# Feed-forward halves joined, the last layer's rounding shared with GpSimd and its last tile halved, the first ternary weights turned by DMA

## The chip, the core and the metric

The kernel runs on one core of a Trainium2 chip. Its engines run side by side, each with an instruction queue of its own: TensorE (PE, matrix products and transposes), VectorE (DVE), ScalarE (ACT), GpSimd (Pool) and SyncE (SP, which here only issues DMA transfers). They wait for each other through semaphores. The metric is the device time of one execution, in microseconds; lower is better.

## The reference, cut

Four transformer layers over x (4 x 256 tokens, D = 256), each an attention-like block and a feed-forward block behind a layer norm:

```python
x = x + _L0_xattn_ref(_layernorm(x), token ids, ctx, ctx, ctx)   # l0x: gated experts chosen by token id
x = x + _L0_ffn_ref(_layernorm(x), w1, w3, w2)                   # l0: ternary weights, SiLU gate
x = x + _L1_xattn_ref(..., w, u, _layernorm(x), ctx)             # wkv: a recurrence along the tokens
x = x + _L1_ffn_ref(_layernorm(x), ...)                          # l1 (shared expert) and the MoE
x = x + _L2_xattn_ref(_layernorm(x), ctx, ...)                   # l2x: attention on quantised values
x = x + _L2_ffn_ref(_layernorm(x), w1, w2, w3)                   # l2: ternary weights, sigmoid gate
x = x + _L3_xattn_ref(_layernorm(x), ctx, ...)                   # l3x: linear attention
x = x + _L3_ffn_ref(_layernorm(x), gate_w, up_w, down_w)         # l3: block-quantised to fp8 steps
```

Ternary weights are `clip(round(w / mean(abs(w))), -1, 1)`, so -1, 0 or 1 times one scale. The last layer quantises activations and weights in blocks of 32:

```python
def _mx_dequant(t):
    blocks = t.reshape(rows, feat // 32, 32)
    scales = maximum(max(abs(blocks), -1) / 448, 1e-30)
    q = (blocks / scales[..., None]).astype(float8_e4m3fn).astype(float32)
    return (q * scales[..., None]).reshape(rows, feat)
gate = _mx_linear(x2d, gate_w); up = _mx_linear(x2d, up_w)
out = _mx_linear(silu(gate) * up, down_w)        # the hidden values are quantised again
```

## The kernel before

Activations stand turned (D on the partitions, 1024 tokens along the row) and are worked on in two halves of 512 tokens. The code is a program written out by hand for each engine; the order in it is the order in which that engine runs, and each engine's queue is strictly in order.

**Feed-forward blocks.** `ffn(s)` stands once for each of PE, ACT and DVE and serves l0x (8 units a half), l0 (6), l1 (3) and l2 (6). A unit i is 128 rows of the hidden layer: PE makes the two products w1 and w3 (below: w(i)), ACT applies the activation, DVE multiplies (`gate`), and PE's `down(i)` adds the unit's share of the output in PSUM banks 4 and 5. `down` lags behind w by `lag` units: 1, or 2 in the blocks in `SPLIT` (l0, l2). There the activations are cut into a high part (ACT, `hidden_high`, `ln_high`) and a low part (DVE, `hidden_low`, `ln_low`) and each product is made with both. A half ends with its last `lag` down products; then DVE adds the output to x (`add_y`, which increments `x_ready`), and only behind that does PE begin the next half. `down(0)` of a half waits for the addition of the half before, since it overwrites the banks.

**Norms inside.** The layer norms of the next half and of the next block's first half are done inside a block, in steps placed by `ln_steps` at given units: PE makes the mean, DVE subtracts (`xc`), ACT squares (`sq`), PE makes the variance (`var`), ACT the root (`sd`, with a table load of 1.28 us each way), DVE `diag`, PE `rows`, DVE `xn`, and in split blocks ACT and DVE the two `parts`.

**Ternary weights.** `ternary` is a list of pieces that DVE runs between the units of l0x (for l0) and of the MoE (for l2): absolute sums, and from piece 7 on the codes, written over the fp32 weights. For l0, PE then turns the weights with 36 transposes behind l0x (`pe_turn(pe, "l0")`), while ACT and DVE copy them out of PSUM in turn (`copy_out`). For l2, Pool casts the codes to bf16 behind DVE's last piece, SP issues three DMA transposes, and ACT copies the results into place behind the attention, ahead of l2.

**Last layer.** 1024 tokens are 8 tiles of 128. DVE's `mx_quant` is a chain: block maxima (tensor_reduce), scale, reciprocal, multiplication, the exponent bits by a tensor_scalar, another tensor_scalar, then an addition and a subtraction of a power that round, and a multiplication back. The tokens of the first half are quantised at once, those of the second in two pieces of two tiles, behind product(1) and product(2). For the hidden values of tile t, PE makes gate and up (`gate_up(t)`), ACT the SiLU, DVE `product(t)` and the chain up to the rounding, Pool the multiplication back (L893), PE turns them (`hidden_turned(t)`), ACT copies them (`hidden_copied`), PE makes `down(t)`, DVE adds the residual (`result(t)`) and SP stores. PE's order is hidden_turned(t), down(t-1), gate_up(t+2); all down products use bank 6, so down(t) waits for result(t-1).

## Time and profile before

| | us |
|---|---|
| median of three runs | 1064.69 |
| lowest, highest | 1057.3, 1065.52 |
| the profiled execution | 1067.97 |
| its span, first to last instruction | 1066.2 |
| PE busy | 874.2 |
| DVE busy | 737.8 |
| ACT busy | 459.8 |
| Pool busy | 147.8 |

The mean granted TensorE clock over the span is 0.834 of full speed. The two levels are 1.2 and 2.4 GHz; through most of the attention of layer 2 (from about 593 to 794 us) it is the lower one. The chain of work that ended last is 51% PE, 26% DVE, 9% ACT, 5% DMA.

How to read it: the timeline lists an engine's instructions in order of time, with runs of equal ones merged, and in brackets how long the engine idled before and what ended last then. A program matmul on fp32 operands shows as two MATMUL rows. L900 is PE's `mm`, L463 the transposes of `pe_turn`; a helper's line is shared by its callers, so the place in time tells which call it is. Idle time costs something only where the chain passes.

### The profile page before, as it was taken

The page shows a single profiled execution, that of the slowest core. Times are in us where ns is not written, and L with a number is a line of the kernel's source. Part 1 is how long each engine was busy: PE and PEld are TensorE (multiplying, and loading weights), DVE is VectorE, ACT ScalarE, POOL GpSimd, SP SyncE. Part 2 cuts the span into 40 slices and gives each one's busy share as a digit, 9 for nine tenths or more (in the row PEclk, how much of TensorE's full clock was granted, in tenths as well). Part 3 has the DMA queues.
Part 4 walks back from the last instruction along what each step waited for, and adds up shares of the span by engine and source line. Part 5 has one row for each costly group of instructions (what it writes and reads, how often), then busy time and mean ns, then how long its engine had stood idle before and what let it go on. Part 6 is the DMA issues. An engine that isn't in the chain of part 4 may idle for free.

```text
span 1066.2 us, 11685 instructions
## 1 busy us (share of the span) xinstructions
PE 874.2 (82%) x4250; PEld 517.8 (49%) x4250; DVE 737.8 (69%) x968; ACT 459.8 (43%) x694; POOL 147.8 (14%) x230
## 2 busy tenths in 40 slices
PE   5999884489799999988999567777788898878796
PEld 3444562244655555554555233434355566644555
DVE  2774558964457787788487987888864436659773
ACT  2213435642324422222223688989964435422110
POOL 1000000000013443236030111111101000001111
PEclk9999886579989999989999655555559979889898
DMA  8500002100122220330036799877760000000000
GB/s 268 175 0 1 1 0 44 23 3 6 21 44 44 40 36 12 67 51 0 1 45 113 146 152 162 150 138 127 139 93 30 1 0 1 1 0 1 10 10 20
DMA packets 206908, 57.96 MB, mean 54 GB/s; under 512 B 187694, under 2 KB 205188, under 8 KB 206852
## 3 DMA queue, kind: packets, MB, share of 16 engines
q1 hardware_dynamic: 206740, 57.05, 28.4%
q8 instruction: 34, 0.56, 0.2%
q10 hardware_dynamic: 112, 0.17, 0.1%
q14 instruction: 22, 0.18, 0.1%
HBM read 20.62 MB, written 1.05 MB: 20 GB/s over the span
## 4 chain that ended last, share of the span: by engine, by line
PE 51%; DVE 26%; ACT 9%; issue 7%; DMA 5%; POOL 1%; ACTq 1%; POOLq 0%; DVEq 0%
PE ps L900 47%; DMA arena<-xc 4%; DVE arena L2493 3%; ACT xc L1800 3%; ACT arena L1810 1%; PE ps L463 1%; DVE arena L2123 1%; PE ps L1030 1%; DVE xn_t L1940 1%; PE ps L1342 1%; DVE xc L2295 1%; ACT arena_split L1717 1%; DVE arena L2502 1%; DVE sq L2404 1%; DVE sq L2401 1%
## 5 line engine op out<-in xcount | busy, mean ns | idle before, releaser
L900 PE MATMUL ps<-arena 128*128 128x16 f16 (+7 forms) x1760 | 269.4, 324 | 66.5 <-ACT xc L1800 29.9
L900 PE MATMUL ps<-arena_split 128*128 128x512 f32 (+5 forms) x736 | 202.4, 439 | 27.5 <-DVE arena_split L1961 14.6
L900 PEld LDWEIGHTS ps<-arena 128*128 128x128 f16 (+4 forms) x1760 | 133.2, 130 | 177.6 <-issue 82.5
L900 PEld LDWEIGHTS ps<-arena_split 128*128 128x128 f32 (+5 forms) x736 | 136.0, 198 | 99.3 <-issue 39.5
L2493 DVE TENSOR_REDUCE arena<-ps 128x1 f32<-128x1024 f32 x128 | 152.4, 1220 | 28.1 <-PE ps L900 26.4
L1800 ACT ACTIVATE xc<-ps,arena 128x1024 int16<-128x1024 f32 x128 | 153.3, 1203 | 25.2 <-POOL arena L876 20.8
L900 PE MATMUL ps<-sq,arena 128*64 128x256 f32 (+3 forms) x256 | 80.9, 515 | 8.3 <-DVE sq L2404 8.3
L876 POOL TENSOR_SCALAR arena<-arena 128x1 f32<-128x1 f32 x128 | 33.9, 265 | 210.6 <-DVE arena L2493 210.6
L1584 ACT ACTIVATE act_buf<-ps 128x512 f32<-128x512 f32 (+2 forms) x34 | 20.3, 597 | 95.2 <-PE ps L900 95.1
L837 POOL TENSOR_SCALAR arena<-arena 128x512 f32<-128x512 f32 x12 | 23.0, 1921 | 248.3 <-DVE arena L2317 248.3
L900 PEld LDWEIGHTS ps<-sq,arena 128*64 128x64 f32 (+3 forms) x256 | 30.1, 166 | 43.6 <-issue 31.2
L900 PE MATMUL ps<-mean_w,sq 128*128 128x1 f32 x240 | 33.3, 269 | 19.4 <-ACT sq L1549 19.4
L900 PE MATMUL ps<-x_t,mean_w 128*128 128x512 f32 x64 | 39.7, 753 | 8.4 <-DVE x_t L2145 4.7
L900 PEld LDWEIGHTS ps<-mean_w,sq 128*128 128x128 f32 x240 | 33.1, 219 | 27.7 <-ACT sq L1549 25.7
L893 POOL TENSOR_TENSOR arena<-arena 128x1024 f32<-128x1024 f32 x8 | 15.3, 1911 | 219.0 <-DVE arena L2060 219.0
L463 PE MATMUL ps<-ident,arena 128*128 128x128 f32 (+5 forms) x158 | 27.4, 322 | 16.1 <-DMA arena<-in_x 6.7
L900 PE MATMUL ps<-xn_t,arena 128*128 128x256 f32 (+2 forms) x112 | 37.6, 488 | 0.2 <-ACT arena L1844 0.2
L2233 DVE TENSOR_TENSOR hid_buf<-ps,act_buf 128x512 f32<-128x512 f32 (+2 forms) x18 | 12.4, 690 | 36.0 <-ACT act_buf L1584 34.8
L2301 DVE TENSOR_TENSOR arena_split<-xc,arena_split 128x1024 fp32r<-128x1024 f32 x16 | 21.9, 1366 | 18.5 <-ACT arena_split L1717 18.5
L463 PEld LDWEIGHTS ps<-ident,arena 128*128 128x128 f32 (+5 forms) x158 | 21.2, 165 | 26.3 <-issue 10.7
L1708 ACT ACTIVATE act_buf<-ps 128x512 f32<-128x512 f32 x16 | 9.6, 599 | 56.4 <-PE ps L900 56.4
L900 PE MATMUL ps<-rsd_diag,ones 128*128 128x512 f32 x32 | 22.6, 796 | 13.6 <-DVE rsd_diag L1934 13.5
(287 smaller groups left out, 1328.5 us busy)
## 6 DMA issues: line engine op xcount, KB each, us to landing
arena<-in_L_ffn_w SPq DMA_DIRECT2D x4, 640.0 KB, 6.0
arena_split<-arena_split SPq DMA_DIRECT2D x59, 32.0 KB
arena<-xc SPq DMA_TRANSPOSE x96, 3.3
arena<-in_x SPq DMA_DIRECT2D x1, 1024.0 KB, 5.7
arena<-in_ctx SPq DMA_DIRECT2D x1, 1024.0 KB, 8.2
arena<-in_L_xattn_Wkv SPq DMA_DIRECT2D x2, 512.0 KB, 4.0
arena<-in_L_ffn_gate_w SPq DMA_DIRECT2D x1, 1024.0 KB, 10.3
arena<-in_L_ffn_up_w SPq DMA_DIRECT2D x1, 1024.0 KB, 12.8
```

Of the source, the lines that this page charges most:

```text
L463: last = pe.transpose(ps[0:m, 6 + g % 2, col:col + w], src, ident[0:src.shape[0], 0:src.shape[0]])
L837: step(pool.tensor_scalar(qf, qf, 2.0 ** -6, 1.5 * 2.0 ** 20, ALU.max, ALU.mult))
L876: pool.tensor_scalar(A["bias"][:, b:b + 1], A["nm"][:, b:b + 1], A["sq"][:, t, i:i + 1], math.log(255.0), ALU.mult, ALU.add).then_inc(att_ ...
L893: pool.tensor_tensor(v, v, mx_s[:, 0, 32 * (t % 2):32 * (t % 2) + 32].unsqueeze(2).to_broadcast([P, 32, MX_BLOCK]), ALU.mult).then_inc(mx_ ...
L900: return pe.matmul(o, l, r, start=start, stop=stop)
L1030: return pe.transpose(ps[0:m, bank, col:col + n], src, ident[0:n, 0:n])
L1342: last = pe.transpose(ps[:, 7, :].bitcast(BF16)[:, k * P:(k + 1) * P], y[:, k * P:(k + 1) * P], ident_b[:, :])
L1584: act.activation(act_buf[0:r, u % 2, :], ps[0:r, 2 * (u % 2), :], func, scale=1.0 if scale is None else scale[0:r, :]).then_inc(act_ready, 1)
L1800: act.activation(att_y[:, u % 4, :].rearrange("p (a b) -> p a b", a=2), ps[:, score_banks(u), :], ACT.Exp, bias=att_small["bias"][:, u % 3 ...
L2233: return TTN(hid, up, s, ALU.mult)
L2301: TTN(parts[:, n % 2, 1], moe["xe"], parts[:, n % 2, 0], ALU.subtract).then_inc(moe_xl, 1)
L2493: dve.tensor_reduce(A["nm"][:, b:b + 1], ps[:, score_banks(u), :], AX.XY, ALU.max, negate=True).then_inc(att_max, 1)
```

## The change

Five edits:

1. **Halves joined.** In `ffn`, `down` of the last `lag` units of the first half is issued behind w(0) (and w(1)) of the second half. DVE's addition of the first half (`summed(0)`) now stands behind the gate (and the low part) of unit `lag - 1` of the second half. `ln_steps` depends on the half in blocks with six units: the first half's norm starts at unit 0 and its parts come at unit 4 instead of 5; the second half's starts at unit 2 instead of 1.
2. **First ternary weights by DMA.** DVE writes the codes of both blocks straight into bf16 buffers. SP issues three DMA transposes for l0 (`ternary_turned("l0", 1)`) as soon as DVE has finished the codes, and ACT copies the results into place behind units 13 and 14 of l0x's 16. PE's turn and the copies out of PSUM go; PE waits for `weights_fixed` instead. DVE gets three small memsets for the padding.
3. **Second ternary weights.** Pool's casts and memsets go; SP's transposes wait for DVE's pieces.
4. **Last layer, tokens.** The subtraction of the second half's norm is moved into the first half's quantisation, behind its reciprocal. The second half's tokens are quantised in one piece behind product(1), DVE up to the power, Pool the two rounding additions and the multiplication back, ahead of its scaling of tile 2.
5. **Last tile halved.** gate_up(7) makes gate and up of the first 512 columns, then of the second. The two halves go through ACT and DVE apart; the first is rounded and scaled by Pool, the second wholly by DVE. down(6) uses bank 7 and last_down bank 0, so neither waits for a result; down(6) comes ahead of the last tile's turn.

The diff, cut to its core:

```diff
@@ PE: ffn
-                    for i in range(s["n"] - lag, s["n"]):
-                        down(i)
+                        if h * s["n"] + i >= lag:
+                            down(*divmod(h * s["n"] + i - lag, s["n"]))
...
+                for i in range(s["n"] - lag, s["n"]):
+                    down(TH - 1, i)
@@ DVE: ffn
+                        if h and i == ffn_lag(s) - 1:
+                            summed(h - 1)
...
-                    dve.wait_ge(hid_used, s["u0"] + (h + 1) * s["n"])
-                    add_y(h, y_scale).then_inc(x_ready, 1)
+                summed(TH - 1)
@@ ln_steps
+            if n == 6 and h == 0:
+                return dict(mean=0, xc=0, sq=1, var=1, sd=2, diag=2, rows=3, xn=3, parts=4)
             if n == 6:
-                return dict(mean=1, xc=1, sq=2, var=2, sd=3, diag=3, rows=4, xn=5, parts=5)
+                return dict(mean=2, xc=2, sq=3, var=3, sd=4, diag=4, rows=5, xn=5, parts=5)
@@ SP
+            def ternary_turned(name, first):
+                for src, dst, at in zip(ternary_16[name], ternary_back[name], (first, first, first + 1)):
+                    sp.wait_ge(weights_fixed, at)
+                    sp.dma_start_transpose(dst.rearrange("p (a b) -> p a b", b=P), src).then_inc(load[name], 16)
+            ternary_turned("l0", 1)
@@ DVE: ternary
-                        step(STT(w, w, st[0:r, 12 + i_:13 + i_], t, ALU.is_gt, ALU.subtract))
-                    if i == TERN_SUM + 4:
+                        step(STT(into[j], w, st[0:r, 12 + i_:13 + i_], t, ALU.is_gt, ALU.subtract))
+                    if i in (TERN_SUM + 3, TERN_SUM + 4):
                         dve.sem_inc(weights_fixed, 1)
@@ ACT: l0x
+            def ternary_copied(name, wts, h, i):
+                full, src, dst = h // P, ternary_back[name][i], wts[i]
+                act.wait_ge(load[name], 16 * 8)
...
+            def first_ternary(i):
+                for part in {TERN_COPIED: (0, 1), TERN_COPIED + 1: (2,)}.get(i, ()):
+                    ternary_copied("l0", wt_l0, H0, part)
-            ffn(l0x, ACT.Silu)
-            copy_out(act, "l0", False)
+            ffn(l0x, ACT.Silu, between=first_ternary)
@@ PE: l0
-            pe_turn(pe, "l0")
-            evacuated(pe, marks["l0"][1])
+            pe.wait_ge(weights_fixed, 3)
@@ Pool
-            for w, o in zip(w_l2[0:2], ternary_16[0:2]):
...
+                if t == 2:
+                    q = xn_tok[:, 4:8, :].rearrange("p t (a b) -> p (t a) b", b=MX_BLOCK)
+                    pool.wait_ge(xq_ready, 2)
+                    rounded_by(q, mxq[:, 4 * D:8 * D])
+                    back_scaled(q, mx_s[:, 0, 64:96], 32).then_inc(xq_ready, 1)
                 pool.wait_ge(mx_scaled, 24 + t + 1)
+                if t == TT - 1:
+                    rounded_by(v, mxq[:, 0:n * MX_BLOCK])
@@ PE: last layer
-            down(TT - 1)
+            down(TT - 2)
+            last_turned(0)
+            last_turned(1)
+            last_down(0)
+            last_down(1)
@@ DVE: last layer
-            ln_xc_of("l3", 1)
             dve.wait_ge(xt_copied, 2)
-            tokens_quantised(0, 4).then_inc(xq_ready, 1)
+            tokens_quantised(0, between=lambda: ln_xc_of("l3", 1)).then_inc(xq_ready, 1)
...
-            step(tokens_quantised(4, 2))
+            dve.wait_ge(xq_ready, 1)
+            tokens_quantised(1, rounded=False).then_inc(xq_ready, 1)
```

PE, from the last down products of l0x into l0, before. `xn_t,ctx_t` and `hid_buf,ctx_t` are l0x's products, `ident` marks a transpose, `arena_split` the split products of l0, `x_t,mean_w` a mean, `mean_w,sq` a variance:

```order
L900 MATMUL ps<-hid_buf,ctx_t 128x512 x4
L463 MATMUL ps<-ident,arena 128x128 x10
L463 MATMUL ps<-ident,arena 128x42 x2
L463 MATMUL ps<-ident,arena 128x128 x10
L463 MATMUL ps<-ident,arena 128x42 x2
L463 MATMUL ps<-ident,arena 128x128 x10
L463 MATMUL ps<-ident,arena 42x128 x2
L900 MATMUL ps<-arena_split 128x512 x16
L900 MATMUL ps<-x_t,mean_w 128x512 x2
L900 MATMUL ps<-arena_split 128x512 x12
L900 MATMUL ps<-mean_w,sq 128x1 x8
L900 MATMUL ps<-arena_split 128x512 x24
```

and of the change, at the same place:

```order
L926 MATMUL ps<-hid_buf,ctx_t 128x512 x4
L926 MATMUL ps<-arena_split 128x512 x8
L926 MATMUL ps<-x_t,mean_w 128x512 x2
L926 MATMUL ps<-arena_split 128x512 x8
L926 MATMUL ps<-mean_w,sq 128x1 x8
L926 MATMUL ps<-arena_split 128x512 x24
L926 MATMUL ps<-rsd_diag,ones 128x512
L926 MATMUL ps<-arena_split 128x512 x12
L926 MATMUL ps<-arena_split 42x512 x8
L926 MATMUL ps<-arena_split 128x512 x40
```

The transposes are gone; the mean stands behind 8 split products instead of 16, the variance behind 8 more instead of 12; and the last down products of the first half stand among the 40, behind the second half's first w.

Pool, from its last ternary work to the end, before (`arena` is nearly every buffer; the last eight are the scalings of the tiles):

```order
L864 CAST arena<-arena 128x2x704
L868 MEMSET arena 128x128x16
L876 TENSOR_SCALAR arena<-arena 128x1 x128
L882 TENSOR_TENSOR arena<-head_mask,lx_kv 128x1024
L886 TENSOR_TENSOR arena<-head_mask,lx_ks 128x1024
L893 TENSOR_TENSOR arena<-arena 128x1024 x8
```

and of the change:

```order
L885 TENSOR_SCALAR arena<-arena 128x1 x128
L891 TENSOR_TENSOR arena<-head_mask,lx_kv 128x1024
L895 TENSOR_TENSOR arena<-head_mask,lx_ks 128x1024
L900 TENSOR_TENSOR arena<-arena 128x1024 x2
L904 TENSOR_TENSOR arena<-arena 128x1024
L905 TENSOR_TENSOR arena<-arena 128x1024
L900 TENSOR_TENSOR arena<-arena 128x1024 x6
L904 TENSOR_TENSOR arena<-arena 128x512
L905 TENSOR_TENSOR arena<-arena 128x512
L900 TENSOR_TENSOR arena<-arena 128x512
```

Pool now rounds the second half's tokens (two rows, and one of the six that follow) between the scalings of tiles 1 and 2, and at the end the first half of the last tile.

## Rows read from the trace of the kernel before

**Rows 1.** Page: span; one group (instruction, count | busy us, mean ns | idle).

```profile
span 1066.2 us, 11685 instructions
...
L2301 DVE TENSOR_TENSOR arena_split<-xc,arena_split 128x1024 fp32r<-128x1024 f32 x16 | 21.9, 1366 | 18.5 <-ACT arena_split L1717 18.5
```

**Rows 2.** Windows: stretch, length, busy us of PE, PEld, DVE, ACT, POOL; granted clock.

```profile
97.30:104.70 7.40, 5.50 (x37) 3.63 (x36) 4.11 (x7) 2.95 (x6) 0.00 (x0) 1.00 0.00 0
104.70:168.50 63.80, 51.91 (x188) 36.41 (x188) 33.99 (x48) 23.20 (x33) 0.00 (x0) 0.85 0.00 1
811.90:867.90 56.00, 47.88 (x189) 33.82 (x190) 25.84 (x36) 22.12 (x33) 4.27 (x2) 0.93 0.05 15
978.30:986.70 8.40, 7.62 (x19) 3.09 (x17) 8.06 (x10) 1.02 (x1) 0.00 (x0) 1.00 0.00 0
986.70:992.80 6.10, 0.07 (x1) 0.00 (x0) 5.82 (x9) 0.00 (x0) 1.91 (x1) 0.72 0.00 0
```

**Rows 3.** Timeline of PE in l0: start us, us, instruction, idle before.

```profile
114.50 2.64 PE L900 MATMUL ps<-mean_w,sq 128*128 128x1 f32 x16 [1.31 <-ACT sq L1549]
117.00 8.27 PE L900 MATMUL ps<-arena_split 128*128 128x512 f32 x24
...
134.98 8.66 PE L900 MATMUL ps<-arena_split 42*128 42x512 f32 x20 [3.59 <-DVE arena_split L1961]
...
151.26 5.82 PE L900 MATMUL ps<-arena_split 128*128 128x512 f32 x24
...
166.56 1.92 PE L900 MATMUL ps<-arena_split 42*128 42x512 f32 x4 [2.92 <-DVE arena_split L1961]
```

**Rows 4.** Timeline of ACT, end of l0x; copies of turned weights ahead of l2.

```profile
85.71 0.60 ACT L1584 ACTIVATE act_buf<-ps 128x512 f32<-128x512 f32 x1
89.95 0.60 ACT L1584 ACTIVATE act_buf<-ps 128x512 f32<-128x512 f32 x1 [3.64 <-PE ps L900]
...
797.43 1.27 ACT L1823 ACTIVATE arena_split<-arena 128x1280 fp32r<-128x1280 bf16 x1 [5.06 <-PE ps L900]
...
801.91 1.47 ACT L1826 ACTIVATE arena_split<-arena 128x1536 fp32r<-128x1536 bf16 x1
```

**Rows 5.** DMA issues by line: count, KB each where known, median us to landing.

```profile
arena<-arena SPq DMA_TRANSPOSE x15, 4.5
```

**Rows 6.** Timeline of SP: the three transposes of the later layer.

```profile
542.51 6.36 SPq L731 DMA_TRANSPOSE arena<-arena  x3
```

**Rows 7.** Timeline of DVE: first ternary codes' last pass; MoE beside Pool's casts.

```profile
77.01 1.64 DVE L2041 SCALAR_TENSOR_TENSOR arena<-arena 128x1364 f32<-128x1364 f32 x1
...
537.86 2.03 DVE L2301 TENSOR_TENSOR arena_split<-xc,arena_split 128x1024 fp32r<-128x1024 f32 x1 [1.12 <-ACT arena_split L1717]
```

**Rows 8.** Timeline of POOL: an addition in the MoE; scaling of tile 1.

```profile
454.87 1.26 POOL L838 TENSOR_TENSOR arena<-arena 128x512 f32<-128x512 f32 x1
...
972.26 1.91 POOL L893 TENSOR_TENSOR arena<-arena 128x1024 f32<-128x1024 f32 x1 [6.64 <-DVE arena L2060]
```

**Rows 9.** Timeline of DVE in the last layer.

```profile
936.03 1.21 DVE L2052 TENSOR_REDUCE arena<-arena 128x32 f32<-128x1024 f32 x1
...
937.49 0.35 DVE L2054 RECIPROCAL arena<-arena 128x32 f32<-128x32 f32 x1
...
972.94 1.26 DVE L2053 TENSOR_SCALAR arena<-arena 128x16 f32<-128x16 f32 x1
...
1063.61 0.42 DVE L2628 TENSOR_TENSOR arena<-ps,arena 128x256 f32<-128x256 f32 x1 [3.89 <-PE ps L900]
```

**Rows 10.** Timeline of PE in the last layer.

```profile
992.95 1.09 PE L1464 MATMUL ps<-ident,arena 128*128 128x128 f32 x4 [6.18 <-DVE arena L2064]
...
1030.95 10.50 PE L900 MATMUL ps<-arena 128*128 128x256 f32 x32
...
1051.90 1.97 PE L1492 MATMUL ps<-ident,arena 128*128 128x128 f32 x8 [6.11 <-POOL arena L893]
...
1059.86 3.71 PE L900 MATMUL ps<-arena 128*128 128x256 f32 x16 [0.61 <-DVE arena L2628]
```

238 lines of the change are left out of this document (151 added, 87 removed).

## The prediction

> **What bounds the kernel now.** I read the page first: the profiled execution spans 1066.2 us [rows 1]. With the launch around it that execution took 1067.97 us, 3.3 us more than the median of the three runs (1064.69); the sum below is made against the span, and 3.3 is taken off at the end. The kernel is one chain of layers, so I then went through TensorE's (PE's) timeline in the five places that the diff touches, asking at each gap what ended last, and through VectorE (DVE), ScalarE (ACT) and GpSimd (Pool) for the same stretches. Four things stand out. (a) Between the first attention-like block l0x and the feed-forward block l0, 7.40 us are spent on turning w_l0: 5.50 us of PE work, with copies by ACT and DVE between [rows 2]. (b) l0 takes 63.80 us with PE busy for 51.91; l2 takes 56.00 us with 47.88 [rows 2]. The largest gap is where the halves meet: PE idles 3.59 us at 134.98 for the second half's parts [rows 3]. (c) In the last layer PE idles 6.18 us before 992.95, for the second half's tokens, which DVE quantises in two pieces of some 6.1 us [rows 2, 10]. (d) At the very end everything is serial: the last tile's DVE chain, Pool's multiplication, 6.11 us of PE idle before 1051.90, and then two down products [rows 10].
>
> **The granted clock matters in (b).** 24 split matmuls take 8.27 us from 117.00 and 5.82 from 151.26; 20 take 8.66 from 134.98, behind the 3.59 us gap [rows 3]. Only the 1.2 GHz level against 2.4 makes such a difference, and l0 has a mean granted clock of 0.85, l2 of 0.93 [rows 2]. So a gap costs its length and may cost again in what follows.
>
> **The change part by part.**
>
> *Turning of w_l0, -7.4.* PE's 36 transposes and the twelve copies go. PE can start l0 when l0x's last down product ends, if the weights are there. DVE now writes the codes as bf16 in the same pass, so its passes cost what they cost (the last ends at 77.01 + 1.64 = 78.65 [rows 7]); three small memsets are added, hidden, as DVE idles elsewhere in l0x. The three DMA transposes go into SP's queue, where nothing waits then. Issuing three took 6.36 us in the later layer [rows 6], one lands 4.5 us after its issue [rows 5]. If all three started only at 78.65, the last would land at 78.65 + 4.24 + 4.5 = 87.4; the first two start some 5 us sooner, so about 83.3. ACT meets its wait behind 85.71 + 0.60 = 86.3, copies two weights for 2 x 1.27 = 2.5 us and two tails of 84 columns, to about 89.4, and its next SiLU starts at 89.95 anyway, after 3.64 us of idle; the third copy, 1.47 us, stands before the last unit in the same way [rows 4]. So the copies are hidden, with about 0.5 us to spare; all of the 7.40 goes. Bounds: -5.5 (landing at 87.4, and PE late by 1.1 plus some) to -7.4.
>
> *Joined halves.* In l0x both sides of the boundary wait for DVE, which has ternary pieces there, and down(8) now waits for the addition behind another gate: 0. In l1: 0 for the same reason (DVE's routing work ends last). In l0 I walked the new order with durations of the rows: w(i) is 8 matmuls of 5.82/24 = 0.2425, so 1.94; down 0.97.
> - Start of a half: the mean now stands behind w(0) and the variance behind w(1), with no down product between. ACT squares only after it has served w(1), so PE waits about 2.6 us instead of 1.31 [rows 3]: +1.3.
> - Boundary: w(0) and w(1) of the second half stand between w(5) and the last two down products. Instead of 3.59 us and a smaller gap of 1.3 ahead of it, some 1.6 remain (for the second half's parts and the addition): -3.3.
> - Second norm and end: +0.3, and +0.6, since rows(5) now stands behind down(3) with the norm's last DVE step in front of the last hidden part (before: 2.92 at 166.56 [rows 3]).
> - Clock: the 20 matmuls behind the vanished gap would take 4.85 instead of 8.66: -3.8. The drop behind the first variance stays.
>
> l0 together -4.9; I book -4, as a wait of 2.6 us may lower the clock for longer. Bounds: +2 (what the boundary gives, the clock takes) to -9 (no low stretch left). l2 has the same order: gaps -1.8, clock -1.8 at its boundary, +2.1 for its first norm, which ran at full clock before; I book -1.5, between +2 and -6.
>
> *Second ternary, -1.* Pool's casts go. One of them ran beside DVE's low part L2301 at 537.86, which took 2.03 us [rows 7] against a mean of 1.366 [rows 1], on the path; some tenths more around it. Bounds 0 to -1.5.
>
> *Last layer, first tokens, -1.8.* The subtraction of the norm (1.22) now stands behind the block maxima. DVE idled before it, waiting for the mean, and can do the maxima (1.21), the scale (0.2) and the reciprocal (0.35) in that time [rows 9]: -1.8. Bounds -1 to -3.5.
>
> *Second tokens, -2.6.* Before, two pieces of 6.1 us [rows 2]. Now one piece of about 4.5 on DVE and then Pool's two additions and its multiplication. Pool takes 1.91 for the multiplication of 128x1024 and 1.26 for an addition of 128x512 [rows 8]; an addition of 1024 lies between 1.91 and 2.52, I take 2.2. Pool is thus done 6.5 us later. But the two engines shut each other out: DVE's 128x16 tensor_scalar from 972.94 took 1.26 us, to 974.20 [rows 9], and Pool's instruction ended at 972.26 + 1.91 = 974.17 [rows 8]. A reduction and an operation that reads PSUM are not held. So tile 2's chain (8.4 us [rows 2]) beside Pool's three instructions is held for about 2.1 at its first tensor_scalar and 1.5 at its first two-input product. The walk: DVE's piece from 972.2 to 977.3 (0.7 held), Pool to 984.0, tile 2's chain to 989.2, Pool's scaling to 991.2, where PE's hidden_turned(2) starts. It started at 993.8: -2.6. Behind that, tiles follow each other at PE's pace, as before. Were nothing held, it would be -5.2; with additions of 2.52, -2.0.
>
> The Trainium skill (SBUF — State Buffer, "Who interferes with whom") says the same against this change: a DVE instruction in a two-port mode, or with two SBUF inputs while GpSimd reads SBUF, fully blocks against GpSimd, and whoever issues first wins. By it and by the row alike the sum is the held one; who ignores it would put 2.6 us more here and about 1.5 more at the last tile.
>
> *Last tile, -8.9.* Before: chain from 1041.5 to 1049.9, Pool to 1051.85, PE from 1051.90, ACT's copy, down(6) between, down(7) from 1059.86 for 3.71 us, result at 1063.61 [rows 9, 10]. After: gate_up(7) ends at 1030.95 + 10.50 = 1041.45, the last 7.0 us of a row of 32 matmuls [rows 10], and gives both operands of the first 512 columns after half of them, at 1037.9. DVE is free at 1039.15 (tile 6's chain began one tile, 11.2 us, before 1041.5, then a result of 0.42), does the first half without rounding to 1042.7, the second with rounding and scaling: 5.8 us, and 2 held by Pool's rounding of the first, to 1050.5. Meanwhile down(6) runs (own bank, no wait for result(5)) and the first half is turned. The second half's turn 1051.1, copy 1051.75, last_down(0) to 1052.9, last_down(1) to 1054.7: result 8.9 earlier. Bounds: -6 (down products at the low level, and Pool slower) to -10.5 (nothing held).
>
> Sum: -7.4 - 4 - 1.5 - 1 - 1.8 - 2.6 - 8.9 = -27.2, a span of 1039.0, a median of 1064.7 - 27.2 = 1037.5.
>
> **The rivals.**
> 1. *The joined halves give much more* because the clock stays up in both blocks: -9 and -6 instead of -5.5, and the shorter gaps in the last layer give another 1 to 3. Time 1024 to 1031. For: the slow matmuls stand behind gaps. Against: the wait for the first variance grows. 17 in 100.
> 2. *The joined halves give nothing* (the new waits for the variance lower the clock for as long as the old boundary did) and Pool's sharing gives 0 to 1: -7.4 - 1 - 1.8 - 0.5 - 7 = -18, time 1045 to 1049. 14 in 100.
> 3. *ACT stalls in l0x*: ACT's queue is in order, so a late transpose delays SiLU, gate and down. It begins to cost at a landing of 86.8 and would eat (a)'s gain at 94. Then 1044 to 1055. Against: a landing of 4.5 us in a stretch without other traffic. 4 in 100.
> 4. *Slower than before*: the new waits, smaller but more regular, keep the granted clock at 1.2 GHz through l0 and l2. By 8.66/4.85 a matmul stretch then takes 1.79 times as long; PE is busy for 51.9 + 47.9, some 90 at full clock, so +0.79 per microsecond. From 27.2/0.79 = 34 us at the low level on, more than now, all the gain is eaten; with 60 the time is 1085. For: the clock drops behind waits. Against: PE's total idle time in both blocks falls. 2 in 100.
> 5. *The change doesn't do what it says*: the instructions do move on every engine in the built order, so this can only be that moved work was never on the path: within 5 us of before. 1 in 100.
>
> **How the numbers follow.** Forecast: 62 in 100, its own range 1032 to 1044. The range that holds 8 in 10 takes rival 1 down to 1027 and rival 2 up to 1048. One per cent, about what a measurement of this kernel tells from no change, is 10.6 us, a bound at 1054: faster 95, within 3, slower 2 in 100.
>
> **What would show each step.** No PE transposes between l0x and l0, and l0's first matmul within 1 us of l0x's last; ACT's copies between 86 and 92 with no wait for DMA before them. In l0 and l2 no gap over 1.5 us at the boundary, but one of 2 to 3 us before the first variance; granted clock of l0 above 0.9. In the MoE, L2301's instruction back under 1.4. In the last layer a DVE tensor_scalar of 2 us or more beside Pool's additions, PE's gap before hidden_turned(2) near 5 us, and the last result about 9 us sooner against the start of gate_up(7). The prediction is wrong if the clock in l0 falls below 0.85, or if Pool's additions take over 3 us each.

## The result, and the profile after

The changed kernel takes 1033.74 us, median of four runs (1032.08 to 1034.88), against 1063.64 before (1057.3 to 1065.52, four runs): a ratio of 0.9728, 95% interval 0.9684 to 0.9772. The forecast was 1037.5 in a range from 1027 to 1048, so direction and size were right: 29.9 us were saved where 27.2 were expected. In a second comparison the same kernel had a ratio of 0.9712 (0.968 to 0.9743), 1035.47 against 1066.77.

The profiled execution spans 1029.6 us at a granted clock of 0.844 (before: 1066.2 [rows 1], 0.834). I cut both executions at the same instructions: l0's first matmul, then the mean matmuls that open the next norm behind l0, at the end of the mixture of experts (MoE), at the end of the attention of layer 2, behind l2, and in the last layer for its second half. The windows view gives per row: stretch, length, busy time (and instructions) of PE, PEld, DVE, ACT, POOL, granted clock, DMA share, GB/s. First l0 and l2 of the kernel before, in these cuts:

```profile
104.72:169.80 65.08, 51.91 (x189) 36.39 (x189) 35.23 (x50) 23.20 (x33) 0.00 (x0) 0.85 0.00 1
797.67:871.47 73.80, 61.63 (x239) 41.84 (x239) 34.26 (x47) 32.22 (x45) 4.27 (x2) 0.90 0.04 11
```

The windows of the changed kernel, all seven:

```profile
0.00:97.44 97.44, 81.22 (x229) 40.35 (x229) 56.08 (x81) 29.61 (x39) 3.31 (x16) 0.95 0.45 133
97.44:155.37 57.93, 47.64 (x190) 32.61 (x188) 36.19 (x51) 23.16 (x33) 0.00 (x0) 0.94 0.00 1
155.37:542.51 387.14, 336.14 (x1282) 191.79 (x1283) 282.52 (x436) 133.39 (x214) 84.43 (x68) 0.91 0.19 30
542.51:779.88 237.37, 175.36 (x1669) 95.49 (x1667) 199.31 (x208) 189.00 (x294) 33.84 (x128) 0.59 0.77 137
779.88:849.67 69.79, 60.08 (x239) 40.70 (x239) 33.88 (x47) 32.03 (x45) 4.21 (x2) 0.93 0.04 12
849.67:907.86 58.19, 49.47 (x236) 38.91 (x237) 35.71 (x36) 28.86 (x41) 0.00 (x0) 0.94 0.00 1
907.86:1029.60 121.74, 107.92 (x376) 67.38 (x374) 88.78 (x107) 24.83 (x31) 24.79 (x13) 0.92 0.03 9
```

Before, the seven stretches took 104.7, 65.1, 388.1, 239.8, 73.8, 61.5 and 133.2 us. The differences are -7.3, -7.2, -0.9, -2.4, -4.0, -3.3 and -11.5, together -36.6. That is 6.7 more than the medians' 29.9: the profiled execution of before (1067.97 us) was 4.3 us over its median, and that of the changed kernel (1032.08) 1.7 under. Two rows in which no edit was meant to act show where some of it lies. The fourth stretch, which holds the attention of layer 2, took 236.7 to 237.9 us in some profiled executions of the kernels below and 239.5 to 240.3 in the others, whatever was edited; before had 239.8, after 237.4. The sixth, the attention-like block of layer 3, took 57.6 to 60.2 in the changed kernel and those below, and 61.5 before, for which there is one profile only.

How the rows of the prediction look now (timeline of PE, l0 of the changed kernel; start, duration, line, count, idle time before it and what ended it):

```profile
97.44 2.42 PE L926 MATMUL ps<-arena_split 128*128 128x512 f32 x8
...
105.67 2.14 PE L926 MATMUL ps<-mean_w,sq 128*128 128x1 f32 x16 [2.24 <-ACT sq L1603]
107.67 7.20 PE L926 MATMUL ps<-arena_split 128*128 128x512 f32 x24
...
122.38 2.81 PE L926 MATMUL ps<-arena_split 128*128 128x512 f32 x11 [0.65 <-DVE arena_split L2034]
...
130.73 1.16 PE L926 MATMUL ps<-arena_split 128*128 128x512 f32 x4 [0.25 <-DVE x_t L2026]
...
137.70 1.95 PE L926 MATMUL ps<-mean_w,sq 128*128 128x1 f32 x16 [1.30 <-ACT sq L1603]
139.51 5.79 PE L926 MATMUL ps<-arena_split 128*128 128x512 f32 x24
...
147.85 1.20 PE L926 MATMUL ps<-arena_split 128*128 128x512 f32 x4 [1.24 <-DVE arena_split L2041]
...
151.98 2.07 PE L926 MATMUL ps<-arena_split 42*128 42x512 f32 x4 [2.92 <-DVE arena_split L2041]
```

The 36 transposes are gone; l0 begins at 97.44, 1.4 us after the start of l0x's last down product. Before, the halves' meeting had the wait of 3.59 us [rows 3] and one of 1.28 ahead of it:

```profile
130.19 1.20 PE L900 MATMUL ps<-arena_split 128*128 128x512 f32 x4 [1.28 <-DVE arena_split L1961]
```

Of these 0.65 and 0.25 remain, but the wait for the first variance is 2.24, and the 24 matmuls behind it still take 7.20 us, not 5.8.

### The profile page after: what moved, and what is told of

It is laid out like the page before. It is cut to its first block, busy times and chain, and to the rows that moved or that the text cites. A ratio compares the mean times of both kernels' runs of the same rounds, so it can differ in the third digit from the quotient of the medians.

```text
span 1029.6 us, 11600 instructions
## 1 busy us (share of the span) xinstructions
PE 857.8 (83%) x4214; PEld 507.2 (49%) x4214; DVE 732.5 (71%) x964; ACT 460.9 (45%) x695; POOL 150.6 (15%) x227
## 4 chain that ended last, share of the span: by engine, by line
PE 51%; DVE 26%; ACT 10%; issue 7%; DMA 5%; POOL 1%; ACTq 1%; DVEq 0%; SPq 0%; POOLq 0%
PE ps L926 48%; DMA arena<-xc 5%; DVE arena L2589 3%; ACT xc L1869 3%; ACT arena L1879 1%; DVE arena L2219 1%; PE ps L1057 1%; DVE xc L2391 1%; ACT arena_split L1786 1%; DVE sq L2500 1%; DVE sq L2497 1%; PE ps L472 1%; DVE arena L2598 1%; DVE xn_t L2020 1%; DVE arena L2133 1%
## 5 line engine op out<-in xcount | busy, mean ns | idle before, releaser
L926 PE MATMUL ps<-arena 128*128 128x16 f16 (+7 forms) x1760 | 270.0, 325 | 65.1 <-ACT xc L1869 30.2
L926 PE MATMUL ps<-arena_split 128*128 128x512 f32 (+6 forms) x736 | 196.9, 431 | 18.9 <-DVE arena_split L2041 5.8
L926 PEld LDWEIGHTS ps<-arena_split 128*128 128x128 f32 (+6 forms) x736 | 132.4, 193 | 90.3 <-issue 40.6
L926 PEld LDWEIGHTS ps<-sq,arena 128*64 128x64 f32 (+3 forms) x256 | 30.0, 166 | 43.4 <-issue 31.4
L900 POOL TENSOR_TENSOR arena<-arena 128x1024 f32<-128x1024 f32 (+1 forms) x9 | 17.5, 1948 | 189.4 <-DVE arena L2157 189.2
L926 PE MATMUL ps<-x_t,mean_w 128*128 128x512 f32 x64 | 36.5, 700 | 8.5 <-DVE x_t L2241 4.8
L2329 DVE TENSOR_TENSOR hid_buf<-ps,act_buf 128x512 f32<-128x512 f32 (+2 forms) x18 | 12.4, 690 | 33.6 <-ACT act_buf L1638 33.3
L1786 ACT ACTIVATE arena_split<-xc 128x1024 fp32r<-128x1024 f32 x16 | 16.9, 1058 | 39.3 <-DVE xc L2391 39.3
L926 PE MATMUL ps<-xn_t,ctx_t 128*128 128x512 f32 x64 | 32.9, 643 | 1.4 <-DVE xn_t L2020 1.4
L1369 PE MATMUL ps<-ident_b,xc 128*128 128x128 bf16 x256 | 32.7, 307 | 0.7 <-ACT xc L1869 0.7
```

The lines of the kernel that those rows point to most:

```text
L900: return pool.tensor_tensor(v, v, scale.unsqueeze(2).to_broadcast([P, n, MX_BLOCK]), ALU.mult)
L926: return pe.matmul(o, l, r, start=start, stop=stop)
L1369: last = pe.transpose(ps[:, 7, :].bitcast(BF16)[:, k * P:(k + 1) * P], y[:, k * P:(k + 1) * P], ident_b[:, :])
L1786: act.activation(moe["xe_parts"][:, n % 2, 0], moe["xe"], ACT.Copy).then_inc(moe_xh, 1)
L2329: return TTN(hid, up, s, ALU.mult)
```

## The experiments

Each kernel was timed beside the kernel before on one chip; runs of one group share it. Times are medians, with the ratio to before and its 95% interval; a profiled execution of each was cut at the same instructions.

| kernel | us | before | ratio | interval |
|---|---|---|---|---|
| halves apart | 1044.46 | 1067.84 | 0.9797 | 0.9737-0.9856 |
| variance later | 1016.95 | 1067.84 | 0.9541 | 0.9506-0.9576 |
| w_l0 turned by PE | 1040.83 | 1067.84 | 0.9754 | 0.9722-0.9787 |
| last tile whole | 1044.02 | 1067.84 | 0.9792 | 0.9751-0.9832 |
| DVE rounds | 1033.14 | 1062.88 | 0.9720 | 0.9688-0.9752 |
| Pool only scales | 1034.66 | 1062.88 | 0.9728 | 0.9690-0.9765 |
| casts on Pool | 1035.26 | 1062.88 | 0.9742 | 0.9692-0.9791 |
| variance later, hidden part first | 1015.95 | 1062.88 | 0.9559 | 0.9515-0.9604 |
| these two, and Pool only scales | 1015.78 | 1066.77 | 0.9532 | 0.9506-0.9557 |
| busy wait | 1032.28 | 1066.77 | 0.9680 | 0.9637-0.9722 |
| changed again | 1035.47 | 1066.77 | 0.9712 | 0.9680-0.9743 |
| busy waits that fit | 1027.39 | 1066.78 | 0.9634 | 0.9593-0.9674 |

### Halves apart

A tuple of the joined blocks decides in `ffn` on all three engines and in `ln_steps`; here it is empty.

```diff
-                        if h * s["n"] + i >= lag:
-                            down(*divmod(h * s["n"] + i - lag, s["n"]))
+                        if down_after(s, h, i, lag):
+                            down(*down_after(s, h, i, lag))
...
+            if n == 6 and s["name"] not in JOINED:
+                return dict(mean=1, xc=1, sq=2, var=2, sd=3, diag=3, rows=4, xn=5, parts=5)
```

> The changed kernel with every feed-forward block's halves apart again (down products, rounding parts, addition and norm steps as before the change); all else stays changed. The prediction's sum (gaps, and the clock only at the boundary): l0 4.0 longer, l2 1.5 longer, l0x the same: 1033.7 + 5.5 = about 1039. Rival, the clock carries further: in the two profiled executions l0 was 7.2 shorter, l2 3.4, the attention-like block l3x behind l2 4.1 (granted clock .85 against .94), and l0x 0.5 longer; if all of that hangs on the join, the time is 1033.7 + 14 = about 1048, and l3x is back at 65 us. Rival, the join gives nothing and the clocks only scatter from one execution to the next: 1034 within 2, with l3x near 61.

Measured: 1044.46, that is 0.9797 of before against 0.9712 and 0.9728 for the changed kernel, so 7 to 9 us. Its windows for l0 and l2:

```profile
97.23:160.99 63.76, 50.62 (x190) 35.04 (x188) 36.46 (x51) 23.18 (x33) 0.00 (x0) 0.87 0.00 1
786.16:858.97 72.81, 60.11 (x238) 40.35 (x239) 34.16 (x47) 32.14 (x45) 4.26 (x2) 0.93 0.04 11
```

Its PE timeline at l0's boundary:

```profile
126.22 7.26 PE L938 MATMUL ps<-arena_split 42*128 42x512 f32 x20 [3.60 <-DVE arena_split L2054]
```

The changed kernel's two profiles have 57.93 and 59.54 for the first stretch and 69.79 and 68.61 for the second. The join is thus worth 4.2 to 5.8 in l0 and 3.0 to 4.2 in l2, together 8.9 and 8.4 in the two pairings, where 5.5 was booked. Four more profiles, of kernels below with the same code in both blocks, have 58.0 to 60.6 and 68.5 to 69.7; against them it is 6.5 to 10.0. Of the kernel with the halves apart there is one profile, and its four times fall into 1038.9 and 1040.6 on one side and 1048.3 and 1048.4 on the other. Without the join the 3.6 us gap is back, and the 20 matmuls behind it take 7.26 us instead of the 4.85 that 24 matmuls in 5.82 [rows 3] would make of them. l3x took 58.8 us here, so its difference from before is not the join's; that part of the larger theory fell, and the 3.3 us of that block stay unexplained. l0x took 35.7 and 35.8 us between the two means inside it, apart and joined.

The split of the gain comes from the same rows. PE idles 63.76 - 50.62 = 13.1 us of l0 with the halves apart and 57.93 - 47.64 = 10.3 joined (59.54 - 49.26 = 10.3 again in the second profile, with 49.26 its PE busy time there): 2.9 of waits. The rest, 3.0 or 1.4, is PE busy for less time with the same matmuls: the clock. In l2 the idle time falls from 12.7 to 9.7 or 9.1, and the busy time hardly.

### Variance later

```diff
-return dict(mean=0, xc=0, sq=1, var=1, sd=2, diag=2, rows=3, xn=3, parts=4)
+return dict(mean=0, xc=0, sq=1, var=2, sd=2, diag=2, rows=3, xn=3, parts=4)
-return dict(mean=2, xc=2, sq=3, var=3, sd=4, diag=4, rows=5, xn=5, parts=5)
+return dict(mean=2, xc=2, sq=3, var=4, sd=4, diag=4, rows=5, xn=5, parts=5)
```

> The changed kernel; only TensorE takes the variance of a norm one unit later in l0 and l2 (behind w(2) and down(0) instead of w(1); in the second half behind w(4) instead of w(3)). If the new waits are what the joined halves still pay, the two waits of 2.24 and 2.15 us for the first variance go below 0.5, and the two of 1.30 and 1.23 for the second vanish: -1.7 - 1.2 in each block, about -5.5 by gaps alone, and -8 if the clock behind them rises too (24 matmuls in 5.82 instead of 7.2): 1028 or 1026. Rival: the wait only moves. ScalarE waits for the variance in front of its next SiLU, the second half's parts come later and the gap shows at the boundary and at the end instead: 1033 to 1034.

Measured: 1016.95, 17 to 19 us less than the changed kernel and twice what the bolder theory gave. Its windows of l0 and l2:

```profile
97.69:148.22 50.53, 45.04 (x191) 31.49 (x189) 36.27 (x51) 22.97 (x33) 0.00 (x0) 0.97 0.00 1
772.85:834.28 61.43, 55.97 (x238) 38.46 (x239) 33.89 (x47) 31.92 (x45) 4.22 (x2) 0.97 0.04 14
```

PE's timeline at the first variance of l0, in the second half and at the end:

```profile
106.89 1.84 PE L926 MATMUL ps<-mean_w,sq 128*128 128x1 f32 x16
108.59 3.03 PE L926 MATMUL ps<-arena_split 128*128 128x512 f32 x12
...
129.03 6.13 PE L926 MATMUL ps<-arena_split 128*128 128x512 f32 x24
...
144.99 1.91 PE L926 MATMUL ps<-arena_split 42*128 42x512 f32 x4 [2.93 <-DVE arena_split L2041]
```

Both waits for the variance are gone, and in their place came one of 0.31 us, for a hidden part ahead of the first variance: ScalarE got its variance in time. l0 is 7.4 us shorter than in the changed kernel's profile, l2 8.4. PE's idle time in l0 fell from 10.3 to 5.5, more than the 3.5 of the two waits, because the waits for hidden parts behind them shrank as well (1.24 to 0.37, 0.65 to 0.32). Its busy time fell from 47.64 to 45.04 with the same matmuls: 24 in 6.13 us, 12 in 3.03, and none of its split matmuls is slow. My expectation had counted the two waits and the two stretches behind the first variance; it had left out the low stretch behind the second variance in l2 (7.26 us in the changed kernel), and the waits that depend on these. The two later kernels with this edit have the same rows: in all three no matmul stretch behind a variance is slow, in l0 or in l2.

### w_l0 turned by PE

```diff
-            pe.wait_ge(weights_fixed, 3)
+            pe_turn(pe, "l0")
+            evacuated(pe, marks["l0"][1])
             ffn(l0)
```

VectorE writes these weights in place again, and the DMA transposes and ScalarE's copies of them go.

> The changed kernel with w_l0 turned by TensorE again (36 transposes behind l0x, twelve copies by ScalarE and VectorE; no DMA transposes of it). The sum: +7.4, 1041. Rival: the turns kept TensorE busy and the clock up, and without them l0 starts behind the gap at l0x's end at a lower clock; then their removal gave less, +4 to +6, 1038 to 1039.5, and l0 itself is shorter than the 56.7 us of the changed kernel.

Measured: 1040.83, +5.4 to +7.1 by medians; in the profile l0's first matmul stands 34.8 us behind the second of the two means inside l0x instead of 27.0, which is 7.8. From the first of these means to the second it is 35.8 us in the changed kernel, where VectorE has the memsets, and 35.5 here, so 7.5 are left. l0 itself was not shorter: 61.5 us against 57.9 to 60.6 in the six profiles that have the changed kernel's code there. The sum's term stands and the rival falls. That the DMA path is hidden is seen in the changed kernel. Its timeline of SP, the three issues:

```profile
74.37 6.87 SPq L707 DMA_TRANSPOSE arena<-arena  x3
```

Its timeline of ScalarE, the first copy, the next SiLU and the last copy:

```profile
86.73 1.26 ACT L1667 ACTIVATE arena_split<-arena 128x1280 fp32r<-128x1280 bf16 x1
...
90.48 0.60 ACT L1638 ACTIVATE act_buf<-ps 128x512 f32<-128x512 f32 x1 [1.00 <-PE ps L926]
90.97 1.48 ACT L1663 ACTIVATE arena_split<-arena 128x1536 fp32r<-128x1536 bf16 x1
```

The copies start with no wait for a DMA, and the next SiLU still idles 1.00 us, waiting for PE.

### Last tile whole

```diff
-            return {TT - 2: 7, TT - 1: 0}.get(t, 6)
+            return 6
...
-            down(TT - 2)
-            last_turned(0)
-            last_turned(1)
-            last_down(0)
-            last_down(1)
+            down(TT - 1)
```

With it go the halved product, SiLU and copy, and Pool's rounding in the last tile, and all down products use one bank again: the run takes back the halving and the banks together.

> The changed kernel with the last tile whole again: one product, one turn, one copy, Pool only multiplies, the down products share one bank. The sum: +8.9, the traces say +9.4, so 1043, with the last result 32.7 us behind the start of gate_up(7) instead of 23.2. Rival: part of that came from a higher granted clock at the end (.95 against .91 in the last stretch) and not from the halving: then +5 to +7, 1039 to 1041, with the down products of the last tile at 16 in 3.7 us in either.

Measured: 1044.02, +8.5 to +10.3. Its timeline of PE:

```profile
1006.37 10.50 PE L924 MATMUL ps<-arena 128*128 128x256 f32 x32
...
1027.32 1.97 PE L1518 MATMUL ps<-ident,arena 128*128 128x128 f32 x8 [6.11 <-POOL arena L900]
1029.09 5.72 PE L924 MATMUL ps<-arena 128*128 128x256 f32 x16
```

Its timeline of DVE, the last result:

```profile
1039.15 0.42 DVE L2726 TENSOR_TENSOR arena<-ps,arena 128x256 f32<-128x256 f32 x1 [3.89 <-PE ps L924]
```

The result is 32.8 us behind the start of gate_up(7), as it was before (32.7 from [rows 9, 10]). The changed kernel's PE at the same place:

```profile
1003.74 10.50 PE L926 MATMUL ps<-arena 128*128 128x256 f32 x32
```

The changed kernel's DVE, held by Pool in the second half of the tile, and the last result:

```profile
1017.26 1.39 DVE L2149 TENSOR_TENSOR arena<-arena 128x512 f32<-128x512 f32 x1
1018.68 1.15 DVE L2151 TENSOR_SCALAR arena<-arena 128x512 int32<-128x512 int32 x1
...
1026.95 0.42 DVE L2736 TENSOR_TENSOR arena<-ps,arena 128x256 f32<-128x256 f32 x1 [3.81 <-PE ps L926]
```

Now it is 23.2 us: -9.4 to -9.6 where -8.9 was booked. In the whole tile down(6) stands behind the 6.11 us wait and takes 5.72 us, partly at the low level, where the same 16 matmuls take 3.63 a tile earlier; halved, it is done before. That is 2.1 of the 9.5, and it was in the sum, which was made from rows with that wait. DVE's product of 0.69 us took 1.39 and its tensor_scalar of 0.43 took 1.15 beside Pool: 1.4 us held, where 2 were expected.

### DVE rounds, Pool only scales

In the first kernel GpSimd has nothing of the second tokens:

```diff
-            tokens_quantised(1, rounded=False).then_inc(xq_ready, 1)
+            tokens_quantised(1).then_inc(xq_ready, 2)
```

> The changed kernel; only the second tokens of the last layer are rounded and scaled back by VectorE (three more instructions of 1.23 us there), and GpSimd has nothing of them. If the two engines shut each other out, as read in the trace of the changed kernel (a product of 1.23 us took 2.93, a tensor_scalar of 0.69 took 2.29, one of 0.18 took 0.74: 3.9 us held), the sharing gave nothing: VectorE ends tile 2's chain within 0.5 us of before and the time stays at 1034. Rival: these three instructions are long for a reason of their own (PSUM, the tile's place), and stay long; then 3.7 us more on the path, 1037.5.

In the second it keeps the multiplication alone:

```diff
-                    rounded_by(q, mxq[:, 4 * D:8 * D])
                     back_scaled(q, mx_s[:, 0, 64:96], 32).then_inc(xq_ready, 1)
...
-            tokens_quantised(1, rounded=False).then_inc(xq_ready, 1)
+            tokens_quantised(1, scaled=False).then_inc(xq_ready, 1)
```

> The changed kernel; VectorE rounds the second tokens itself (two more instructions of 1.23) and GpSimd only multiplies them back, once. If the hold comes from pairs of instructions that meet, this one meets tile 2's product from PSUM and its maxima, which were not held beside GpSimd's additions: nothing is held, tile 2's chain ends at +2.5 - 3.3 - 0.5 = 1.3 us sooner than in the changed kernel, the time is about 1032.5. Rival: GpSimd's multiplication holds the chain as long as it runs, wherever it stands (1.9 to 2.8 us): +1, 1035.

Measured: 1033.14 and 1034.66, neither to be told from the changed kernel. The traces can tell. First DVE of the changed kernel in tile 2's chain:

```profile
954.22 2.93 DVE L2149 TENSOR_TENSOR arena<-arena 128x1024 f32<-128x1024 f32 x1
957.18 2.29 DVE L2151 TENSOR_SCALAR arena<-arena 128x1024 int32<-128x1024 int32 x1
```

Pool of the changed kernel beside it, the second rounding addition and the multiplication:

```profile
953.71 2.35 POOL L905 TENSOR_TENSOR arena<-arena 128x1024 f32<-128x1024 f32 x1
956.14 2.77 POOL L900 TENSOR_TENSOR arena<-arena 128x1024 f32<-128x1024 f32 x1
```

The first of these DVE instructions with nothing on Pool:

```profile
961.30 1.23 DVE L2143 TENSOR_TENSOR arena<-arena 128x1024 f32<-128x1024 f32 x1
```

Pool's timeline in the other kernel, its single multiplication:

```profile
958.75 1.91 POOL L900 TENSOR_TENSOR arena<-arena 128x1024 f32<-128x1024 f32 x1 [5.74 <-DVE arena L2156]
```

DVE's timeline there, the tensor_scalar that was held before:

```profile
962.96 0.69 DVE L2150 TENSOR_SCALAR arena<-arena 128x1024 int32<-128x1024 int32 x1
```

They take 1.23 and 0.69 us, not 2.93 and 2.29: the long durations come from GpSimd's instructions that run at that time. 954.22 + 2.93 ends at 957.15, while Pool's second addition ended at 956.06 and its multiplication was issued at 956.14. A multiplication that meets DVE's product from PSUM and its maxima holds nothing (both take 1.22) and itself takes 1.91 instead of 2.77. The Trainium skill (SBUF — State Buffer, "Who interferes with whom") says that an operation with two SBUF inputs contends with a GpSimd instruction that reads SBUF, and that a reduction never does. The trace agrees: 2.93 us against 1.23 for the first, 1.22 beside GpSimd for the second.

From the second mean of the last layer to gate_up(4) it is 65.65 us in the changed kernel's profile and 65.67 in its second, 65.65 once more in a kernel below, 64.0 to 64.3 in seven other kernels that share the rounding in the same way, 63.24 with DVE alone, and 61.95 with Pool only scaling. So sharing the rounding lost 0.8 to 2.4 us.

The holds alone are not the reason. DVE is held for 3.9 us in the changed kernel, but 0.56 of it is a small tensor_scalar (0.74 us instead of 0.18) beside Pool's scaling of tile 1, and it is held as long with DVE alone. The other 3.3 us are less than the 3.7 of work that DVE is spared, and PE turns tile 2 sooner with the shared rounding, 56.90 to 57.12 us behind the mean against 57.46. The turn in the changed kernel, and with DVE alone:

```profile
964.76 1.97 PE L1520 MATMUL ps<-ident,arena 128*128 128x128 f32 x8 [3.06 <-POOL arena L900]
```

```profile
968.55 1.09 PE L1514 MATMUL ps<-ident,arena 128*128 128x128 f32 x8 [1.51 <-POOL arena L900]
```

With DVE alone PE waits twice, 1.83 and 1.51 us, and behind that the turn takes 1.09 us and the 16 matmuls of down(1) 3.63. With the shared rounding it waits once, 3.04 to 3.06 us, and they take 1.97 and 4.12 to 5.78. The loss is in PE's clock behind the one longer wait.

### Casts on Pool

```diff
             pool.wait_ge(weights_fixed, 5)
+            for w, o in zip(w_l2[0:2], ternary_16["l2"][0:2]):
+                o = o.rearrange("p (a b) -> p a b", b=D)
+                step(pool.tensor_copy(o[:, 0:full], w[:, 0:full]))
...
```

> The changed kernel; VectorE writes the second ternary weights in f32 in place and GpSimd casts them to bf16, as before the change. The sum: +1.0, 1034.7, with one low-part subtraction of about 2.0 us beside a cast. Rival, from the two profiled executions: the stretch around it was 2.6 us shorter after the change, so all of that comes back, 1036.3. Rival: that stretch only scatters, and nothing comes back, 1033.7.

Measured: 1035.26 (1032.61 to 1040.1), nothing that the times can tell. Its timeline of Pool, a cast:

```profile
525.11 1.25 POOL L879 CAST arena<-arena 128x1280 bf16<-128x1280 f32 x1
```

Its timeline of DVE, the low part beside that cast:

```profile
525.41 2.03 DVE L2409 TENSOR_TENSOR arena_split<-xc,arena_split 128x1024 fp32r<-128x1024 f32 x1 [1.12 <-ACT arena_split L1796]
```

The same instruction took 1.23 us in the changed kernel and 2.03 before beside the same cast [rows 7]. The stretch from l0 to the MoE took 387.9 us here against 387.0 to 387.2 in six profiles without the casts, 388.0 to 388.4 in five others without them, and 385.9 in one. So 0.8 us of hold is shown. That the whole stretch gains 1.0 would fit before's 388.1, but it is within what that stretch scatters, and is not shown.

### Hidden part first

On top of the later variance, in l0 only:

```diff
+                        if (s["name"], h, i) == ("l0", TH - 1, s["n"] - 1):
+                            hidden_low(s, h, i)
                         if h and i == ffn_lag(s) - 1:
                             summed(h - 1)
```

> The kernel with the later variance; in l0 the last unit's low hidden part is made right behind the one before it, ahead of the piece of the last layer's scales and of the norm's last product (3.6 us of VectorE work between them now). TensorE's gap of 2.93 us before the last down product goes, and the addition starts as soon as that VectorE work is done: 1.8 us sooner, 1015.1 against 1016.95. Rival: what follows is bound by VectorE, whose work is the same, so nothing moves by more than its idle time before the addition (2.00 us) allows; and if the norm's product, now later for the work behind it, takes it back, 1017.

PE's timeline at the end of l0, the next block's mean:

```profile
146.12 3.78 PE L926 MATMUL ps<-x_t,mean_w 128*128 128x512 f32 x4 [3.13 <-DVE x_t L2026]
```

The 2.93 us before the last down product are gone (PE now idles 3.13 before the mean, for the addition, instead of 1.32), and that mean stands at 146.12 against 148.22, 1.9 us sooner counted from l0's start. The median, 1015.95 (1011.72 to 1021.03), doesn't resolve that. The mechanism is shown by the trace, the gain in time is not.

### All three together

> The kernel with the later variance and the low hidden part first, and VectorE rounding the second tokens with one multiplication left to GpSimd. From the traces of the single edits, each measured between the same instructions: 15 to 17 for the variance, 1.9 for the hidden part, 2.1 for the tokens (from the last layer's second mean to gate_up(4) 61.95 us against 64.05 in the kernels that share the rounding): 1033.7 - 16.8 - 1.9 - 2.1 = about 1013. Rival, the edits are not independent (the clock, raised in one place, is lost in another): 1016 or more.

1015.78 us (1015.37 to 1017.9), 0.9532 of before against 0.9541 for the later variance alone: no difference. In its profile the last layer has the 118.0 us that Pool's single multiplication promised (121.7 in the changed kernel's profiles, 120.1 in most kernels with the same code there), and l0 with 48.6 us has the shorter end, but the input phase ahead of l0x was 1.9 us longer. It beats both kernels, before by 51 us and the changed one by 18 to 20, and the later variance alone carries nearly all of that. The 1013 that the single edits added up to were missed by 3 us; the input phase accounts for 1.9 of it in the profile, and the rest is open.

### Busy waits

Does the clock fall because PE waits, or in these blocks whatever it does? Useless matmuls are put in front of the wait, behind the one for the bank:

```diff
+                if (name, h) in (("l0", 1), ("l2", 1)):
+                    pe.wait_ge(xn_ready, n)
+                    for _ in range(4):
+                        mm(ps[:, ln_row_bank(name, h), :], mean_w[:, :], x_t[:, 0, tok(h)], True, True)
                 pe.wait_ge(ln_sq, n + 1)
```

> The changed kernel; TensorE gets four useless matmuls (mean_w by x_t, 1.9 us together at full clock, their output is overwritten) in front of its wait for the first variance in l0 and in l2, so that it waits as long as before but is busy. If the granted clock falls because TensorE idles there, the 24 matmuls behind the wait take about 5.9 us instead of 7.2 and 7.07, and the time is 1 to 4 us shorter although work was added: 1030 to 1033. Rival: the clock follows something else in these blocks (all the split matmuls draw more, whatever the waits): the 24 matmuls stay at 7.1 to 7.4, the time at 1034 or a little more.

> The changed kernel itself once more, beside the two others on one chip, as the base that they are compared with and to see how much one execution's stretches scatter: 1033.7 within 2. Its profile should show the first variance's wait of 2.24 us in l0 and 24 matmuls of about 7.2 us behind it again; the stretch from the MoE's end to l2, which took 237.4 us in one profile and up to 240.3 in others with the same code, may take either.

PE's timeline in l0 with the busy wait (the useless matmuls have two rows each):

```profile
103.90 3.60 PE L926 MATMUL ps<-x_t,mean_w 128*128 128x512 f32 x8
...
109.04 5.82 PE L926 MATMUL ps<-arena_split 128*128 128x512 f32 x24
...
139.51 7.37 PE L926 MATMUL ps<-arena_split 128*128 128x512 f32 x24
```

The same of the changed kernel again:

```profile
109.14 7.33 PE L926 MATMUL ps<-arena_split 128*128 128x512 f32 x24
...
141.15 5.79 PE L926 MATMUL ps<-arena_split 128*128 128x512 f32 x24
```

With PE busy up to the variance, the 24 matmuls took 5.82 us instead of 7.33. In l2 it is the same:

```profile
806.85 5.70 PE L926 MATMUL ps<-arena_split 128*128 128x512 f32 x24
```

This is more than scatter: in the seven profiles in which PE waits idle there, 2.24 us in l0 and 2.15 in l2, the fourteen stretches behind the wait took 7.07 to 8.25 us, without one exception. The added work, 3.60 us and twice what I had supposed, delayed the variance by 1.0 us, and still the second half's mean came 31.4 us behind the first's instead of 33.6 (32.0 in the changed kernel's first profile). The time is 1032.28 against 1035.47 on the same chip; the intervals overlap. So idleness is part of the cause. The Trainium skill (TensorE: Matmul & The Clock Gate, Part 1) says that a monitor sets the clock by how busy PE has been lately, and here trace and rule agree. But the stretch behind the second variance took 7.37 us in this kernel and 5.79 in the changed one, behind waits of 1.31 and 1.30. Here scatter can't be ruled out: the kernel with the whole last tile, which is the changed kernel up to there, took 7.35 behind the same 1.30.

The last kernel uses two matmuls for the first waits and one for the second ones, so that nothing is delayed.

> The changed kernel with useless matmuls that fit inside the waits this time: one took 0.9 us in the run before (four took 3.60, not 1.9 as supposed), so two (1.8 us) stand in front of the wait for the first variance in l0 and l2 (2.24 and 2.15 us), and one in front of the wait for the second (1.30 and 1.24). The waits last as long as before and nothing is delayed. If the low level behind them comes from TensorE's idleness, all four stretches of 24 matmuls take 5.7 to 5.9 us (7.33, 5.79, 7.33 and 7.35 in the changed kernel's second profile): 1.5 us three times, about 4.5 shorter than 1035.5, 1031; what is then left to the 18 us of the later variance is the waits themselves and more. Rival: idle waits of 0.3 us that stay are enough for the low level, or it has another cause: some or all of the four stretches stay above 7, 1034 to 1036.

Its timeline of PE in l0:

```profile
105.65 2.14 PE L926 MATMUL ps<-mean_w,sq 128*128 128x1 f32 x16 [0.52 <-ACT sq L1608]
...
139.50 5.80 PE L926 MATMUL ps<-arena_split 128*128 128x512 f32 x24
```

In this profile 0.52 us of idle time are left before the first variance in l0, 0.38 to 0.45 before the three others, and all four stretches (7.20, 5.80, 7.16, 7.37 us) are as in the changed kernel: the rival's picture. Yet the median of six runs is 1027.39 (1026.0 to 1031.26), and the profiled execution was the slowest of them; the ratio's interval, 0.9593 to 0.9674, lies just below that of the changed kernel, 0.968 to 0.9743. That the clock was better in the other five would fit, but no trace shows it. What length of wait costs the clock is therefore open. That the clock stays up when the first wait is filled with work up to its end is shown by one profile with two such stretches, and that it stays up when both waits are moved away, by three profiles.

## Why the prediction was right

**Turning of w_l0, -7.4:** right. 7.3 between the profiles, 7.5 against the kernel that turns by PE, 5.4 to 7.1 by medians, no wait of ScalarE for a DMA, 1.0 us to spare.

**Joined halves, -4 and -1.5:** the mechanism was right, the size too small; 8.4 and 8.9 us by the kernel with the halves apart, of which l0 has 4.2 to 5.8 and l2 3.0 to 4.2 (6.5 to 10.0 with the four other profiles). The step that was mis-sized is the walk through the boundary and what follows. Item by item in l0, from [rows 3] and the rows above, before against changed: first variance +0.93 (walk +1.3), boundary 4.87 to 0.90, so -3.97 (walk -3.3), second norm 0 (walk +0.3), end 0 (walk +0.6). Idle time thus fell by 2.9 where the walk had 1.1. The clock's part was forecast as 3.8 and was 4.3 between the two profiles, 1.4 to 3.0 against the kernel with the halves apart. On top I had booked -4 where the walk gave -4.9. In l2 the idle time fell by 3.0 to 3.6 against 1.8. Behind the first variance the clock stayed low in l0 and fell in l2, where it had been full before (24 matmuls in 5.73 us, now 7.07), as forecast. The granted clock of l0 rose to 0.94 and 0.91, above the 0.9 that I had named.

**l0x and l1, 0:** right, with the addition as the last wait at l0x's boundary (1.60 us); l1 took 32.8 us from its first matmul to the transposes behind it, against 32.9 before. l0x's 0.2 to 0.3 us of extra time stand with the kernels that have the three memsets on DVE, and not with the one that turns w_l0 by PE, which is joined too; I had booked these memsets as hidden.

**Second ternary, -1:** 0.8 shown at the one instruction; the rest lies within scatter.

**First tokens, -1.8:** right; from the norm's mean to the turn of the first quantised tokens 9.73 us against 11.5 before. 1.0 of it was left at tile 0's turn (31.69 against 32.70 us), since gate_up(0) took 8.05 us instead of 7.28.

**Second tokens, -2.6:** half right. The held durations came near the forecast (3.9 us in all, with 0.7, 2.1 and 1.5 booked), and the turn of tile 2 came 4.0 us sooner, 2.2 without the first tokens' 1.8. But of the 2.2 only 0.3 to 1.9 us was left at gate_up(4): the matmuls behind the remaining gap ran partly at the low clock. That gap, forecast near 5 us, was 3.06. And the step failed in what it credited: I had priced the sharing against nothing, not against DVE doing the same additions. The gain comes from quantising in one piece; the sharing gave 0.3 to 0.6 us at tile 2's turn and lost 0.8 to 2.4 by gate_up(4), by way of PE's clock, which this term had left out.

**Last tile, -8.9:** right, -9.4 to -9.6.

**The sum:** -27.2 was forecast and -29.9 measured, with the terms as the runs have them 7.5 + 8.6 + 0.8 + 1.8 + 0.3 to 1.9 + 9.5 = 28.5 to 30.1: 3 us more in the joined halves, 0.7 to 2.3 less in the second tokens. That these two errors go against each other is luck. Rival 1 (the joined halves give much more) was right about the side, but not about its reason: most of the surplus is shorter waits and not the clock, and the last layer gave nothing more. Rival 2's reason, the new wait for the variance, is real and was the dearest thing of all that was tried: 17 us with all that hung on it, though it did not outweigh the gain.

## What to carry over

When halves or tiles are joined, look again at each wait that the moved work used to cover: here a norm's variance taken one unit too early cost more than half of what the whole change gave, with stretches partly at the low clock and smaller waits behind its 2.2 us. Before work goes from VectorE to GpSimd, price it against VectorE doing it itself, and place GpSimd's instruction beside VectorE's reads of PSUM and its reductions; its product of two SBUF inputs and its large tensor_scalar were held here. See also whether the new order gathers TensorE's short waits into one longer one. Read gains of a few microseconds from stretches between the same instructions, beside a stretch that nobody edited, since the median of one and the same kernel differed here by 1.7 us (the changed one) and by up to 5 (before) from one comparison to the next.
